# A fused transformer kernel: another order of Pool's work in the stage between its two attentions, and later reciprocals

## The reference

```
x = x + attn_block(layernorm(x))
x = x + ffn_block(layernorm(x))

attn_block(x):   h = layernorm(x) * g + b;  q, k, v = split(h @ Wqkv);  rotate q and k
                 a = causal softmax(q k / sqrt(8)), 16 heads of 8;  x = x + (a v) @ Wo
                 return x + gelu((layernorm(x) * g2 + b2) @ W1 + b1) @ W2 + b2'
ffn_block(x):    attention of 16 heads without a mask, with biases;  x1 = layernorm(x + attn_out)
                 8 experts of width 512, the best 2 for each token, weighted;  layernorm(x1 + moe)
```

## Time and profile before

| | |
|---|---|
| median of three runs | 1614.51 us (1611.68 to 1620.99) |
| the profiled execution, first to last instruction (span) | 1605.8 us |
| median less span | 8.7 us |
| PE busy in the span | 1393.0 us (87%) |
| DVE, ACT, Pool busy | 1220.5, 1141.7, 478.8 us |
| stage of this case | about 525 to 677 us |
| PE, DVE, ACT, Pool busy from 505 to 677 us | 134.1, 88.8, 90.5, 82.8 us of 172 |
| mean granted clock there | 0.94 |

### The profile page before, as it was taken

One profiled execution on the slowest core, in us unless ns is written; L12 is line 12 of the kernel. 1 busy time (PEld: TensorE's weight loads), 2 busy tenths in 40 slices (PEclk: granted clock), 3 DMA queues, 4 the chain that ended last, 5 costly groups with the idle time before them and its releaser, 6 DMA issues.

```text
span 1605.8 us, 36099 instructions
## 1 busy us (share of the span) xinstructions
PE 1393.0 (87%) x13425; PEld 603.7 (38%) x13425; DVE 1220.5 (76%) x1846; ACT 1141.7 (71%) x2357; POOL 478.8 (30%) x786
## 2 busy tenths in 40 slices
PE   5769999999998887559999999999999999899940
PEld 2323333333333455202222222322222235889830
DVE  6788888888882466599999999999999962432434
ACT  7628888888888555309999998899888997434421
POOL 5313333333333556200000002200221334332455
PEclk9859999999999999759999999999999999999975
DMA  4522112121112344400134412111201312788941
GB/s 137 192 88 74 62 47 69 43 76 56 62 46 74 109 131 133 142 28 11 56 136 149 158 61 82 42 50 51 76 35 33 101 68 90 222 236 259 269 128 57
DMA packets 130255, 158.26 MB, mean 99 GB/s; under 512 B 17312, under 2 KB 103328, under 8 KB 129824
## 3 DMA queue, kind: packets, MB, share of 16 engines
q1 hardware_dynamic: 120864, 130.77, 26.1%
q0 software_dynamic: 9216, 25.18, 4.6%
HBM read 90.90 MB, written 68.96 MB: 100 GB/s over the span
## 4 chain that ended last, share of the span: by engine, by line
PE 44%; DVE 9%; issue 5%; DMA 3%; POOL 3%; ACT 2%; SPq 1%; POOLq 0%; ACTq 0%; DVEq 0%
PE bank L628 16%; PE banks L613 10%; DVE row_max L664 6%; PE banks L585 6%; PE banks L1524 4%; PE banks L1514 4%; POOL probs L1332 2%; DMA qk_parts<-parts 2%; ACT o_sums L724 1%; PE banks L1505 1%; DMA parts<-sorted_in 1%; PE banks L337 0%; PE banks L1416 0%; DMA expert<-expert_rows 0%; PE banks L1469 0%
## 5 line engine op out<-in xcount | busy, mean ns | idle before, releaser
L664 DVE TENSOR_REDUCE row_max<-banks 128x2 f32<-128x1024 f32 (+3 forms) x896 | 933.8, 1103 | 62.4 <-PE banks L585 34.4
L709 ACT ACTIVATE probs<-banks 128x512 f32<-128x512 f32 (+3 forms) x1792 | 875.5, 552 | 117.0 <-PE banks L613 94.5
L628 PE MATMUL bank<-probs,v_ones 128*32 128x256 f32 (+2 forms) x6656 | 524.3, 387 | 12.0 <-ACT o_sums L724 10.8
L585 PE MATMUL banks<-k_work,q_work 48*128 48x512 bf16 (+3 forms) x1792 | 359.5, 377 | 60.7 <-DVE row_max L664 47.0
L613 PE MATMUL banks<-q_work,k_work 51*128 51x512 bf16 (+3 forms) x1792 | 377.2, 368 | 10.8 <-ACT probs L709 9.8
L613 PEld LDWEIGHTS banks<-q_work,k_work 51*128 51x128 bf16 x1792 | 104.6, 93 | 380.9 <-ACT probs L709 346.9
L628 PEld LDWEIGHTS bank<-probs,v_ones 128*32 128x32 f32 x6656 | 133.8, 108 | 260.6 <-ACT probs L709 173.5
L750 POOL DMA_DIRECT2D heads_out<-o_sums x64 | 36.4, 568 | 470.2 <-ACT o_sums L724 470.2
L2092 ACT ACTIVATE rope<-banks,expert 128x256 f32<-128x256 f32 x184 | 72.2, 475 | 108.0 <-PE banks L1514 108.0
L770 POOL TENSOR_SCALAR_AFFINE_SELECT probs<-probs 128x256 f32<-128x256 f32 x256 | 104.0, 410 | 125.4 <-ACT probs L709 124.7
L585 PEld LDWEIGHTS banks<-k_work,q_work 48*128 48x128 bf16 x1792 | 90.3, 95 | 117.3 <-DVE row_max L664 90.2
(11 more groups left out here) (195 smaller groups left out, 1035.7 us busy)
## 6 DMA issues: line engine op xcount, KB each, us to landing
expert<-expert_rows SPq DMA_DIRECT2D x46, 578.0 KB, 4.5
qk_parts<-parts SPq DMA_DIRECT2D x64, 256.0 KB, 3.4
heads_out<-o_sums POOLq DMA_DIRECT2D x64, 256.0 KB, 3.8
sorted_in<-front SPq DMA_DIRECT2D x21, 512.0 KB, 6.1
q_work<-qk_parts SPq DMA_DIRECT2D x64, 128.0 KB
k_work<-qk_parts SPq DMA_DIRECT2D x64, 128.0 KB
parts<-sorted_in SPq DMA_DIRECT2D x46, 128.0 KB, 4.2
q_work<-qk_parts SPq DMA_DIRECT2D x64, 64.0 KB
```

Source lines behind the costliest of these rows:

```text
L585: last = pe.matmul(to[:, par, 0:width], q[r:r + M0, pair, qt * P:(qt + 1) * P], k[r:r + M0, pair, kh * G:kh * G + width], start=True, stop ...
L628: last = pe.matmul(bank[7][32 * j:32 * j + 32, c0 + c1:c0 + c1 + w], v_ones[i % QB][:, kt, j, :], prob_slots[:, (e + j) % RING, c1:c1 + w] ...
L664: dve.tensor_reduce(row_max[:, :, pair, qt, kh], self.buf_of("chunk", g, c)[:, :, 0:width], AX.X, ALU.max).then_inc(s["chunk_max"], 1)
L709: act.activation(prob_slots[:, e % RING, 0:width], self.ring_bank("exp", e)[:, 0:width], ACT.Exp, scale=SCALE).then_inc(s["exps"], 1)
```

## The change

- Pool's list per turn becomes: root of x, `add_b2` of group i (was: of i+1, one turn ahead), `sum_x`, root of z of group i-1, `low` of i-3, `add_be2` of i-1, `add_bo` of i-1 (was: of i-2).
- `apply_z` waits for `add_bo` of the group before (`zo`) and no longer for the landing of its store.
- SP stores z of group i-1 at the end of turn i, behind the store of x (was: of group i-2, first in the turn).
- The load of the last batch's sums goes from ahead of turn 0 into turn 1 of SP's list, the store of the reciprocals into turn 2, the reciprocals themselves from turn 0 to the end of turn 1 of DVE's list.

```diff
@@ SP @@
-            attend[1].load_sums(sp, B - 1)
-            attend[1].store_reciprocals(sp, B - 1)
             for i in range(GROUPS + 3):
-                if 0 <= i - 2 < GROUPS:
-                    store_z(i - 2)
+                if i == 1:
+                    attend[1].load_sums(sp, B - 1)
+                if i == 2:
+                    attend[1].store_reciprocals(sp, B - 1)
                 if i + 2 < GROUPS:
                     load_heads(i + 2)
...
                 if 0 <= i - 1 < GROUPS:
                     store_x(i - 1)
+                    store_z(i - 1)
                 if LOAD_FROM <= i - 3 < GROUPS:
                     attend[2].load(sp, i - 3 - LOAD_FROM)
@@ Pool @@
                 if i < GROUPS:
                     if i:
                         root(i, 0, "x", "xd")
+                        add_b2(i)
                     sum_x(i)
+                if 0 <= i - 1 < GROUPS:
+                    root(i - 1, 1, "z", "z")
                 if 0 <= i - 3 < GROUPS:
                     proj[2].low(pool, GROUPS + i - 3)
-                if 0 <= i - 2 < GROUPS:
-                    add_bo(i - 2)
-                if i + 1 < GROUPS:
-                    add_b2(i + 1)
                 if 0 <= i - 1 < GROUPS:
-                    root(i - 1, 1, "z", "z")
                     add_be2(i - 1)
+                    add_bo(i - 1)
@@ DVE @@
                 if i + 1 < GROUPS:
                     scale_heads(i + 1)
-                if i == 0:
-                    attend[1].reciprocals(dve, B - 1)
...
                 if 0 <= i - 1 < GROUPS:
                     add_down(i - 1)
+                if i == 1:
+                    attend[1].reciprocals(dve, B - 1)
@@ ACT, apply_z @@
-                    act.wait_ge(mid["z_out"], 16 * n)
+                    act.wait_ge(mid["zo"], n)
```

## The result

The changed kernel takes 1595.42 us in the median of four executions (1592.15 to 1596.51), the kernel before 1614.8 us beside it (1611.68 to 1620.99): a ratio of 0.9894, 95% interval 0.986 to 0.9927. This recorded ratio stands for 17.1 us; the plain quotient of the two medians is 0.9880, 19.4 us. The forecast of 1598.0 is 2.6 us too high, and the range of 1592.5 to 1606.5 holds it. The profiled execution has a span of 1593.1 us at a mean granted clock of 0.94. One of the executions reported further down, of f1, took 1759.29 us at a mean granted clock of 0.72, where all others have 0.90 to 0.94, and is left out of f1's median and ratio; no trace shows why it was slow. In the changed kernel `root` stands at L1214 and L1216, `add_b2` at L1207, `sum_x` at L1222, `add_bo` at L1229, `add_be2` at L1235; the lines of the other engines that are named here have kept their numbers.

The account below looks back on a forecast made before the run. It took a closed ring of ACT and Pool, with a late root of z, to bound the stage between the attentions. Head and turns gain 17.9 us, the tail returns some, leaving 16.4: 1614.5 to 1598, range 1592.5 to 1606.5.

Parts of the forecast that it names:

- The ring: ACT, four Pool instructions, ACT again set the 16.78 us turn; new turn 14.46. D+ counts from the turn's down product.
- projection stall: TensorE's fourth projection (L337) waits 1.41 us for the first rope product; 0.22 would be left with moments 1.19 us earlier.
- The tie with Pool: Next turn's first root gives its offset at D+14.74, `apply_x` wants it at D+14.79; within 0.1 us, so 14.5 taken.
- the root and to L1611 as two terms: Pool's root of z ahead of `low`: `apply_z` 3.43 us earlier, including 1.19 us from DVE's L1611 at 0.17 instead of 1.36.
- hidden behind the root save 0.2 us: ACT's `apply_z`: its three waits for the store of z, removed by waiting on `zo`, cost only 0.2 us beyond the root.
- The head: Start of the stage between the attentions, reciprocals moved: first down product about 531.2, second 543.8 against 547.95, full clock taken.
- The tail: Last down product to attention 2's first row_max: loads issued at D+12.5, 1.6 us later; row_max at D+31.4 against D+29.85.
- the port: Port shared by DVE and Pool: in the new order only L1611 meets the tail of `add_bo`; rope products keep full speed.
- rival C: Attention 2's first phase waits for something that does not move, so its earlier start is lost: 1614.5 us; chance 0.06.
- A: Rival: Pool binds, roots at 1.9 us and L1611 at 1.2 make the turn 16.6 us: 1608.7 us; chance 0.10.
- B: Rival: three Pool additions in a row shut out DVE's rope products, turn 19.6 us: 1623.7 us; chance 0.04.
- D: Rival: more gain, turns of 14.24 us and a tail of 29.8: 1595.3 us or lower; chance 0.06.

Follow-up runs that it names:

- f1: The changed kernel unaltered, run again on a third chip beside the kernel before: 1600.5 us, ratio 0.9902.
- e7: The changed kernel with one more 128x512 addition on Pool in each turn, ahead of `add_be2`, its output unused: 1607.92 us in one execution.
- e10: The changed kernel with `low` put back ahead of the root of z on Pool: 1609.51 us in one execution.
- e2: The kernel before with Pool's root of z ahead of `low` and `apply_z` waiting for `zo` instead of the landing of z: 1621.77 us in one execution.
- e1: The kernel before with only Pool's root of z moved ahead of `low`: 1636.44 us, ratio 1.0142.
- e5: The changed kernel with attention 2's first three loads in turns 5, 6 and 7 of SP's list instead of 8, 9 and 10: 1589.46 us, ratio 0.9861.
- e8: The changed kernel with `apply_z`'s old wait for the landing of z put back beside the new one: 1605.54 us in one execution.
- f2: The changed kernel with attention 2's first three loads in turns 5, 6 and 10, on f1's chip: 1592.33 us, ratio 0.9841.
- e6: The changed kernel with attention 2's first three loads in turns 5, 6 and 10 of SP's list, on chip 2: 1589.72 us, ratio 0.9838.
- e3: The kernel before with only the moves of the sums' load and the reciprocals' store and computation: 1608.16 us, ratio 0.9982.

## Why the prediction was right

**The ring.** Root at D+6.44, `apply_z` at D+7.77 against D+7.78; L1611 at 0.17; projection stall 0.22; turn 14.44 against 14.46 from the sum and 14.5 taken. The tie with Pool that made it 14.5 exists, but falls about 0.1 us on TensorE's side: the offset is out at 600.94, where ACT has waited for one it starts 0.03 us later (608.46 and 608.49), and `apply_x` starts at 601.05, behind hT. e7 shows how thin that is.

**What the prediction did not separate.** It put the whole turn down to the root and to L1611 as two terms of one move. e10 shows that the swap with `low` gives only the L1611 term, and that the rest needs `add_bo` and `add_b2` gone from between; e2 and e1 show that the swap without moving `add_bo` is worth nothing or costs 23 us. The prediction did not say that `add_bo` a turn ahead is a condition for the wait on `zo`; it named the removed wait as "hidden behind the root save 0.2 us". In the kernel before that is right for the first of the three waits only; in the other two the landing held `apply_z` 1.2 and 1.0 us longer than the offset did (offset out at 639.19 and 656.13, `apply_z` at 640.41 and 657.14). For any half of the change it would have misled.

**The head.** First down product 530.56 in a trace whose stage starts 0.62 us earlier, so 531.2 as forecast; second down product 543.16 (543.8 forecast, same shift). That the clock stays full there was a choice, and a lucky one: it did in this trace, e5, e7 and e8, not in f1, f2, e6 and e10, nor in e3 with its equal gap.

**The tail.** Its start was mis-sized: the loads are issued at D+13.54, not D+12.5. The reason is in Pool's and DVE's last turn after:

```profile
636.19 2.13 POOL L383 TENSOR_TENSOR parts<-probs,parts 128x1024 bf16<-128x1024 f32 x1
638.28 2.25 POOL L1235 TENSOR_TENSOR xm<-probs,ln_rows 128x512 f32<-128x512 f32 x1
```

```profile
637.53 1.88 DVE L369 TENSOR_TENSOR probs<-probs 128x1024 f32<-128x1024 f32 x1
```

DVE's addition started at 637.53 beside `low` and takes 1.88 us instead of 1.22; it ends at 639.41, and `add_be2`, begun at 638.28, takes 2.25 instead of 1.26. Each seems to hold up the other, and `add_bo` behind them starts 1 us late. The prediction had such a holding up (what it calls the port) for L1611 and for the root, and not for these two, since in the steady turn they do not meet. The Trainium skill, "SBUF — State Buffer", "Who interferes with whom", calls the shared pair an exclusive lock whose holder blocks the other for the whole instruction; the two lengths fit it within 0.15 us: L369 is 0.66 us longer than alone, and `low` ends 0.79 us after its start; `add_be2` is 0.99 us longer, and L369 ends 1.13 us after its start.

The landing came at D+26.8 against D+26.7 all the same, since it took 13.3 us from the issue, not 14.2; the high part at D+28.1, not D+28.6: it waited for a store of the group that begins at 647.68 behind the loads (the one issued at 648.1, landed 8.6 us later), whose chain the prediction had only by analogy. Two errors of 1.0 and 0.9 us cancelled by luck; the tail was 30.91 against 31.4. That the tail follows the issue of the loads is borne out by e10 and e7: issue at D+11.67, D+13.54, D+15.77, tail 29.02, 30.91, 33.43.

**The end.** Whether a shorter stage shortens the whole was rival C. The span fell by only 12.7 us, since the part behind attention 2's last store is 261.3 us here and 254.4 before; over the twelve traces it lies between 253.5 and 263.6 and does not follow the stage (253.5 with a stage of 126.95, 254.4 with 152.40). The times of many executions are the better witness. Ratio less one, times the median before, beside the difference of the stage from 152.40:

| kernel | e1 | e3 | changed | f1 | e5 | f2 | e6 |
|---|---|---|---|---|---|---|---|
| stage, us | +27.3 | -3.7 | -17.1 | -13.7 | -22.3 | -25.1 | -25.5 |
| time, us | +22.9 | -2.9 | -17.1 | -15.8 | -22.4 | -25.7 | -26.2 |

By the ratios the time follows the stage within some 2 us, and 4 in e1; their intervals reach 4 to 7 us to either side. The plain differences of the medians (+25.7, -2.6, -19.4, -15.1, -21.3, -23.2, -29.4) follow it within 4. C, that nothing arrives, is out; that every microsecond does is not shown that finely. Of the 2.6 us by which the forecast is too high, 0.7 are the stage (17.1 against 16.4), and the rest is within the scatter of the executions. Where the prediction put 8.7 us between span and median and let them stay, the changed kernel has 2.3 between them; its profiled execution took 1594.96 us for a span of 1593.1, so only some 1.9 lie around a span. If as much lay around it before, the remaining 6.8 were a profiled execution faster than the median.

**The rivals.** A (Pool binds) stands about 0.1 us away in the steady turn and was not reached. B (the rope shut out) did not happen: the four rope products took 2.72 us beside `low` (608.41, rope from 606.99). D took its period of 14.24 in turn 2 only. e1 is slower by a mechanism that none of them named, the landing of z behind `low` and `add_bo`; it applies to half of the change only.

## What to carry over

In a hand-ordered ring of engines, an instruction can be moved ahead only as far as the oldest wait of its consumer allows: write down all semaphores that the consumer waits for, with the time at which each arrives in the new order, since the one that was hidden sets the next ring. Look at the small instructions of DVE (0.17 us) that lie beside Pool's long ones; one that grows to 1.36 costs its full length where a chain runs through it. Put loads of the next stage where no store that someone waits for is issued behind them; here that is worth 9.6 us of the stage, more than half of what the change brought.

## What the runs showed of the hardware

**TensorE's clock at the head.** In identical code the granted clock at 526 to 528 us of the trace was 1.00 in the changed kernel's first trace and 0.50 in f1. In turn 1, TensorE idles 1.90 to 1.92 us before the second half of the up products in seven traces with moved reciprocals; the four matmuls then take 1.98 us in the changed kernel, e5, e7 and e8, 2.48 in e3 and e6, and 3.56 in f2. In f1 they take 3.66 after 2.28 us, in e10 3.68 after 2.29, in the kernel before 3.27 after 2.53. An equal gap is no sure sign of the clock, and the head of this stage carries up to 3.4 us (f1 and e10) that an execution takes or leaves. What decides between them is open; no run changed it alone.

**Stores behind loads.** The seven stores of 256 KB issued from 647.7 to 660.3 us, behind loads, landed in 2.7 to 11.2 us, 8.8 in the middle (two of them in 2.7 and 2.8, so standing behind loads is not the whole of it), where those of `x_mid_d` and `z_d`, also of 256 KB but issued ahead of the loads, landed in 2.3. The summary of the transfers after, 640 to 662 us (KB each, median us to landing):

```profile
qk_parts<-parts SPq DMA_DIRECT2D x7, 256.0 KB, 8.8
...
q_work<-qk_parts SPq DMA_DIRECT2D x4, 128.0 KB
...
x_mid_d<-xm SPq DMA_DIRECT2D x1, 256.0 KB, 2.3
z_d<-probs SPq DMA_DIRECT2D x1, 256.0 KB, 2.3
```

The loads themselves, 128 KB or less each and written to 2 or 4 runs of partitions each, go with a low DMA share: 0.19 and 0.25 from 644 to 648 us and 0.22 to 0.27 from 652 to 658, with 0.79 and 0.87 between them while the stores of 647.7 to 649.2 run. The Trainium skill, "DMA: Bandwidth & Descriptors", "Why a DMA increments its semaphore by 16 and not by 1", has a transfer spread over only as many engines as divide its outermost dimension, which roughly agrees with that share (2 or 4 of 16 busy would be 0.13 or 0.25); that it is the reason was not tried by itself.
